# Five engine orders and the PSUM bank of every piece of work, written anew

## What is computed

```
block 0  attention: q, k = elu(.)+1; kv = k^T v per head (16 heads of 8); out = q kv / (q sum k)
         experts:   logits -> top 2 of 8 experts; y = sum of gate * (gelu(xn W1 + b1) W2 + b2), 128 -> 512 -> 128
block 1  attention: softmax(q k^T / 4) v, 8 heads, q and k of 16 features, v summed over its last axis
         experts:   top 1 of 8; x + x expert_w[chosen]
```

## Time and profile before

| | |
|---|---|
| median of three executions | 699.16 us (696.32 to 702.93) |
| profiled execution, first to last instruction | 694.9 us |
| PE busy, with unread matmuls | 602.8 us |
| DVE busy | 484.6 us |
| ACT busy | 390.7 us |
| POOL busy | 334.6 us |

### The profile page before, as it was taken

The page is one execution under the profiler, slowest core; times in us unless marked ns, Lnnn a source line. Parts: engine busy times, 40 slices in busy tenths (PEclk is TensorE's granted clock), DMA queues, the critical chain, the costliest instruction groups (busy, mean ns, idle before and its releaser), DMA issues. The chain is left out here.

```text
span 694.9 us, 11955 instructions
## 1 busy us (share of the span) xinstructions
PE 602.8 (87%) x3825; PEld 385.3 (55%) x3825; DVE 484.6 (70%) x1275; ACT 390.7 (56%) x866; POOL 334.6 (48%) x363
## 2 busy tenths in 40 slices
...
GB/s 338 100 1 0 62 107 152 179 241 258 190 292 322 175 312 262 138 323 199 214 132 193 208 282 245 76 39 188 56 53 1 166 62 190 130 80 34 31 61 30
DMA packets 47037, 106.40 MB, mean 153 GB/s; under 512 B 7056, under 2 KB 22224, under 8 KB 45440
## 3 DMA queue, kind: packets, MB, share of 16 engines
...
q10 hardware_dynamic: 432, 0.34, 0.2%
...
## 5 line engine op out<-in xcount | busy, mean ns | idle before, releaser
L889 ACT ACTIVATE bufa<-PS 128x512 f32<-128x512 f32 x256 | 139.5, 599 | 78.5 <-PE PS L1556 72.0
L1200 DVE TENSOR_REDUCE mxs<-PS 128x2 f32<-128x1024 f32 x128 | 151.2, 1218 | 28.9 <-PE PS L1540 28.1
L848 ACT ACTIVATE bufb<-PS,bufb 128x128 f32<-128x128 f32 x368 | 103.5, 380 | 43.2 <-PE PS L1505 42.9
L1505 PE MATMUL PS<-bufb 128*128 128x128 f32 x736 | 97.2, 281 | 14.0 <-DMA bufb<-in_experts_dram 7.0
L1505 PEld LDWEIGHTS PS<-bufb 128*128 128x128 f32 x736 | 90.5, 195 | 20.9 <-issue 9.0
L1513 PE MATMUL PS<-bufb 128*128 128x128 f32 x736 | 97.3, 281 | 0.4 <-ACT bufb L848 0.3
L701 POOL DMA_INDIRECT bufb<-slots_out,bufb x64 | 62.2, 971 | 68.9 <-DMA bufb<-slots_out,bufb 36.0
L688 POOL DMA_INDIRECT slots_in<-bufb x64 | 67.2, 1049 | 56.9 <-DVE bufb L1146 38.7
L1513 PEld LDWEIGHTS PS<-bufb 128*128 128x128 f32 x736 | 91.3, 197 | 3.8 <-issue 1.4
L1540 PE MATMUL PS<-stk 96*128 96x512 bf16 x256 | 75.2, 386 | 16.1 <-DVE mxs L1200 5.6
L1556 PE MATMUL PS<-stk 108*128 108x512 bf16 x256 | 81.4, 389 | 7.8 <-ACT bufa L889 6.8
...
## 6 DMA issues: line engine op xcount, KB each, us to landing
...
```

The costliest lines, as they stand in the source:

```text
L848: last = nc.scalar.activation(hs[:, n % HR, fc, :], ps[:, P * fc:P * fc + P], ACT.Gelu_apprx_tanh, bias=ws[:, n % WR, F + fc:F + fc + 1])
L889: nc.scalar.activation(probs[:, i % PR, j, :], psum("s2", i, j), ACT.Exp, scale=DH1 ** -0.5)\
L1200: nc.vector.tensor_reduce(mxs[:, gr % 2, 2 * j:2 * j + 2, h], psum("s1", i, j).rearrange("p (c n) -> p c n", c=2), axis=AX.X, op=ALU.max)\
L1505: last = nc.tensor.matmul(ps[:, P * fc:P * fc + P], ws[:, n % WR, P * fc:P * fc + P], xq[:, q % 2, P * x:P * x + P], start=True, stop=True)
```

## The change

Nothing is added to and nothing taken from the pieces: each engine's string holds the same pieces (PE 801, ACT 499, DVE 332, SP 183, POOL 95), in another order. 192 of PE's stand where they stood, 184 of ACT's, 154 of DVE's, 64 of POOL's, 35 of SP's; a PE piece moves by 1.8 places in the mean. 353 of the 669 pieces with a bank have another bank. The unread matmuls keep their number and go with their pieces. Of the many moves, those that the prediction speaks of:

Because the maxima of a group need no longer be taken in the order of their pieces, DVE's `msp` waits for the last user of every bank in its group instead of for the group's last two pieces:

```
+        def last_on_bank(kind, group, it):
+
+            cls, n, k = USE[(kind,) + it]
+            return all(USE[(kind,) + x][2] <= k for x in group if USE[(kind,) + x][1] == n)
...
                 if kind == "msp":
-                    for k in range(2):
-                        emptied(v, "s1", 4 * i + 3, k)
+                    for h in range(4):
+                        for k in range(2):
+                            if last_on_bank("s1", [(4 * i + a, b) for a in range(4) for b in range(2)], (4 * i + h, k)):
+                                emptied(v, "s1", 4 * i + h, k)
```

More of the change, by code:

```diff
@@ L68 @@
     "PE": """
[L69 to L94, removed]
```

267 lines of the change are left out of this document (151 added, 116 removed).

## The result

Four executions of the changed kernel took 708.52 to 711.65 us, median 710.12; four of the kernel before 694.18 to 702.93, median 697.74. The ratio on record is 1.0186 with a 95% interval of 1.0143 to 1.0229 (the quotient of the two medians is 1.0177). The forecast was 683, its range 673 to 697.

The account below looks back on a forecast made before the run. PE, busy 602.8 of 694.9 us, was taken as the bound, with chains of waits from 123 to 303. Gains summing to 16.0 gave a 678.9 us span, 683 on the median's scale; range 673 to 697.

Parts of the forecast that it names:

- Start, 4.0: Up to the second expert tile: moved unread matmuls save 1.5 us, an earlier ACT copy 3.0 less 0.5; 0 to 6.
- So the 4.0 is carried: POOL's chain, 183 to 255 us: keeps the start's 4.0, adds 3.3 before cn3.0.0 and 1.1 before pair 1's gathers; 8.4.
- the forecast's 15.9: 270 to 303 us: cpt.0.0, moved ahead of bga.1.3, ends at 273.8, so cto.0.0 comes 15.9 us earlier.
- The skill's rule there: Shared ports: bn4.3.0's normalisations on DVE could delay cn3.0.0's steps on POOL, making the sum 2 us smaller; none was taken.
- First stacks, 16: 270 to 303 us: cto.0.0, cst.0.0 and its landing come earlier, so s1.0.0 starts at 287 instead of 303.
- where the sum had 4.4: s1.0.0 to ctr.1.0: ctr.1.0 comes only 11.6 us earlier, so the 16 of s1.0.0 are not all kept.
- the 4.4 forecast: ctr.1.0 to bh.3.4: PE's 2.02 us of idle filled before ctr.1.0, plus 2.4 at s1.16.0, bringing the sum to 16.0.
- s1.16.0's wait of 3.14: PE idle before s1.16.0, for a double bank cpv.3.0 held; with cpv.3.0 first, 2.4 of the 3.14 us is saved.
- PE is busy, so the shift passes through: 303 to 440 us: PE is busy 129 of 137 us, so the time gained earlier passes through.
- All other shuffles after 440: I take 0: Reordered scores, exponentials and value products after 440 us: no net change taken, range -8 to +8 us.
- The bound of 12.7 us for banks: After 440 us: more bank hand-overs between PE users cost at most 12.7 us; better order may return up to 17.4.
- SP's queue: Third rival, slower: SP stands at cto.0.0 if cpt.0.0 ends no sooner than 289.7, delaying bh.2.15's weights; 708 us, chance 0.09.

Follow-up runs that it names:

- e10: The changed kernel with group 1's experts (184.7 to 244.3 us) put back to the old order and banks; ratio 1.0198 to the kernel before.
- e12: The changed kernel's orders and banks up to s1.32.0 (480.8 us), the old ones behind; ratio 1.0170 to the kernel before.
- e15: The changed kernel with dn1.2.0 moved behind mx.53.0 on DVE, s1.52.0 and s1.52.1 ahead of pv.12.0 on PE; ratio 1.0270 to the kernel before.
- e1: The changed kernel, orders untouched, its two double banks dealt in turn from s2.16.0 to s1.32.0; ratio 1.0424 to the kernel before.
- e5: The changed kernel, orders untouched, double banks from s1.23.1 on given by whose occupant is emptied first; ratio 1.0312 to the kernel before.
- e6: The changed kernel, orders untouched, single banks from s1.23.1 on given by whose occupant stands first in ACT's order; ratio 1.0163 to the kernel before.
- e18: The changed kernel with old orders and banks from 184.7 to 244.3 us and behind 394.4; ratio 0.9942 to the kernel before.

## Why the prediction was wrong, by its own steps

- **Start, 4.0.** Right within its bounds of 0 to 6, and low: bh.0.2 comes 5.4 us earlier in the mean of the 17 profiles with the new start (4.1 to 7.05; the last is the changed kernel's own, which lies above the bounds and whose clock to there was 0.99 against 0.94).
- **"So the 4.0 is carried", 183 to 255.** Failed. The sum followed POOL alone and never costed PE's and SP's new order of group 1's experts, which loses 11.1 us at bxt.2.0 and still about 4 at s1.0.0. POOL's part came as forecast and better: cn3.0.0 is 10.7 us earlier and no longer behind bn4.3.0. But bga.1.0 then stands 8.35 us for the store byo.1.5, whose products PE finished late: 251.07 instead of 246. With group 1 in the old order (e10) cpt.0.0 comes 15.3 us earlier, against the forecast's 15.9. DVE at bn4.3.0, SP at byo.1.5 and POOL at bga.1.0 of the changed kernel:

```profile
239.23 2.14 DVE L995 TENSOR_SCALAR bufb<-wa,mom,rstd 128x128 f32<-128x128 f32 x8
```
```profile
247.02 0.32 SPq L553 DMA_DIRECT2D slots_out<-bufb  x1
```
```profile
251.07 1.07 POOL L714 DMA_INDIRECT bufb<-slots_out,bufb  x1 [8.35 <-issue]
```

- **The skill's rule there.** The rule that VectorE, in its two-port modes, and GpSimd lock a shared pair of ports (the Trainium skill, SBUF — State Buffer, Who interferes with whom) made no difference at this place: the eight of bn4.3.0 took 2.14 us beside cn3.0.0's steps on POOL, and these took 0.20 to 0.24 us each and the power at their end 1.65, as before. It shows at another: the cast at 450.37 above took 1.37 us while POOL's cpt.5.0 ran (448.45 to 451.70), and ended with it; at 435.80 the same cast took 0.17. s1.28.1 waited 2.05 us behind it, against 1.32 in e10, e12 and e15, where the cast took 0.23 to 0.49. POOL's second step of cpt.5.0:

```profile
449.58 2.12 POOL L752 TENSOR_TENSOR terms<-rest,terms 128x1024 bf16<-128x1024 f32 x1
```

- **First stacks, 16.** cpt.0.0 13.1 and cto.0.0 12.8 earlier, s1.0.0 only 7.75 (5.7 in the mean of ten): the step took the store's 3.95 us as fixed, and it took 8.9. ctr.1.0 gave back 3.3 where the sum had 4.4. ctr.1.0 to bh.3.4 brought 3.5 of the 4.4 forecast, and s1.16.0's wait of 3.14 is gone in all kernels with the new order there; but the old order has -2.4 in the same stretch, so only about 1 us of it is the new order's.
- **"PE is busy, so the shift passes through", 303 to 440.** Failed, and this is the step that turned the sign, with the next: PE's own pieces kept their lead, DVE's did not. DVE lost 7.9 us to mx.24.0 in the new order and 0.8 in the old one.
- **"All other shuffles after 440: I take 0", -8 to +8.** Failed. They cost 5.5 to s1.32.0 and 5.2 more to s1.52.0, where the old order has 0.2 and -2.6. The bound of 12.7 us for banks was near in size, but no change of banks alone brought the time back (e1, e5, e6).
- **The rivals.** The one on the other side, SP's queue, gave 708, close to 710 by luck: its condition was not met, since cpt.0.0 was 13 us early and bh.2.15 only 1.1 us late.

Open: how much of the loss behind 394 is order, how much banks, how much the clock. Behind 430 PE was granted 1.2 GHz for about 29 us in the changed kernel, 17 in the kernel before and 15 in e18. From s1.32.0 to s1.52.0 it was 10 to 21 us in the five kernels with the new order there and 3 to 12 in the eight with the old one (14 in the one profile of before), so some of the difference there goes with the clock; whether the clock is the cause or follows the order's stops no run separates.
